# Graph layer on one core: edge sums with destinations as rows, half of each batch in two fp32r parts, mix by token

## The reference

```python
xn = layernorm(x)                                   # (6250, 256)
# graph part: one message per edge, summed at its destination
all_msg = einsum('nf,rfo->rno', xn, weight)         # 16 relations
gate = sigmoid(einsum('nf,rf->rn', xn, gate_weight))
msg = all_msg[rel, src] * norm * gate[rel, src]     # norm: one number per edge
agg = relu(segment_sum(msg, dst))
# mix: linear attention; it folds into one 256 x 256 matrix M
k, v = inst_norm(xn @ w_k), inst_norm(xn @ w_v)     # 8 heads of 64
dots = k.T @ v                                      # per head, over all nodes
mix = (xn @ w_q) @ dots / n @ w_out + b_out         # = xn @ M + b_out
x = x + agg + mix
# ffn: 8 experts, top 2 by a softmax router
y = layernorm(x)
x = x + y + sum_e combine[:, e] * (gelu(y @ w1[e] + b1[e]) @ w2[e] + b2[e])
```

## Time and profile before

| | |
|---|---|
| median of three runs | 1878.89 us |
| profiled execution | 1881.19 us, span 1878.9 us |
| TensorE matmul busy | 1792.0 us, 95% |
| VectorE busy | 1174.8 us, 63% |
| ScalarE busy | 772.5 us, 41% |
| GpSimd busy | 774.0 us, 41%, all of it from 617 us on but a few us |
| granted TensorE clock, mean | 0.984 |

### The profile page before, as it was taken

One profiled execution on the slowest core, in us unless ns is written; L12 is line 12 of the kernel. 1 busy time (PEld: TensorE's weight loads), 2 busy tenths in 40 slices (PEclk: granted clock), 3 DMA queues, 4 the chain that ended last, 5 costly groups with the idle time before them and its releaser, 6 DMA issues.

```text
span 1878.9 us, 30569 instructions
## 1 busy us (share of the span) xinstructions
PE 1792.0 (95%) x11137; PEld 1604.8 (85%) x11137; DVE 1174.8 (63%) x3496; ACT 772.5 (41%) x1428; POOL 774.0 (41%) x812
## 2 busy tenths in 40 slices
PE   5999999999999799999699999999999999999988
PEld 4887888888888699998689998999899989999988
DVE  6555555444443677676657677676686776767764
ACT  4545556555554433332033333333343342432443
POOL 2000000000000466767776666666566666566600
PEclk8999999999999999999899999999999999999999
DMA  7655777655555764443443333433334333333400
GB/s 221 228 222 216 278 291 283 243 213 219 218 219 209 257 244 142 144 146 113 147 123 113 109 121 89 131 112 110 115 94 135 110 108 109 93 118 114 113 16 17
DMA packets 113913, 296.04 MB, mean 158 GB/s; under 512 B 18120, under 2 KB 73792, under 8 KB 104420
## 3 DMA queue, kind: packets, MB, share of 16 engines
q1 hardware_dynamic: 75236, 189.63, 27.4%
q0 software_dynamic: 38528, 104.46, 19.2%
HBM read 162.70 MB, written 131.32 MB: 156 GB/s over the span
## 4 chain that ended last, share of the span: by engine, by line
PE 87%; DVE 6%; POOL 2%; issue 2%; DMA 1%; SPq 1%; ACT 1%; DVEq 0%; ACTq 0%
PE bank L51 22%; PE bank L53 21%; PE bank L52 21%; PE bank L1337 16%; POOL plain L585 2%; PE bank L1326 2%; PE bank L1402 1%; PE bank L1230 1%; DVE plain L951 1%; SPq L479 1%; PE bank L1442 1%; PE bank L1205 1%; DVE plain L984 1%; PE bank L1383 1%; PE bank L1392 0%
## 5 line engine op out<-in xcount | busy, mean ns | idle before, releaser
L585 POOL DMA_INDIRECT plain<-messages,idxT x784 | 763.2, 973 | 1005.5 <-issue 843.2
L51 PE MATMUL bank<-parts 128*128 128x512 f32 (+2 forms) x2232 | 813.3, 364 | 29.5 <-DVE plain L984 21.3
L53 PE MATMUL bank<-parts 128*128 128x512 f32 (+2 forms) x2232 | 786.3, 352 | 0.0
L52 PE MATMUL bank<-parts 128*128 128x512 f32 (+2 forms) x2232 | 785.6, 352 | 0.0
L51 PEld LDWEIGHTS bank<-parts 128*128 128x128 f32 x2232 | 426.6, 191 | 81.9 <-issue 33.7
L53 PEld LDWEIGHTS bank<-parts 128*128 128x128 f32 x2232 | 425.1, 190 | 55.0
L52 PEld LDWEIGHTS bank<-parts 128*128 128x128 f32 x2232 | 426.6, 191 | 46.3
L1337 PE MATMUL bank<-plain 128*128 128x128 f32 x3136 | 392.7, 280 | 22.1 <-DMA plain<-messages,idxT 18.4
L1337 PEld LDWEIGHTS bank<-plain 128*128 128x128 f32 x3136 | 378.1, 196 | 28.6 <-DMA plain<-messages,idxT 20.7
L1156 ACT ACTIVATE plain<-bank,small 128x512 f32<-128x512 f32 (+1 forms) x208 | 135.1, 662 | 376.8 <-PE bank L53 373.4
L658 DVE TENSOR_SCALAR plain<-bank,plain 128x256 f32<-128x256 f32 x392 | 171.0, 478 | 163.0 <-PE bank L53 109.4
(11 more groups left out here) (150 smaller groups left out, 985.3 us busy)
## 6 DMA issues: line engine op xcount, KB each, us to landing
messages<-plain SPq DMA_DIRECT2D x49, 2048.0 KB, 7.0
parts<-xnT_scratch SPq DMA_DIRECT2D x20, 1024.0 KB, 5.1
xnT_scratch<-parts SPq DMA_DIRECT2D x98, 128.0 KB, 3.2
plain<-messages,idxT POOLq DMA_INDIRECT x784, 2.8
w_parts<-parts SPq DMA_DIRECT2D x32, 256.0 KB, 2.4
parts<-w_parts SPq DMA_DIRECT2D x4, 2048.0 KB, 20.4
plain<-in_x SPq DMA_DIRECT2D x48, 128.0 KB, 7.1
plain<-in_x SPq DMA_DIRECT2D x10, 512.0 KB, 4.4
```

The lines of the kernel that those rows point to most:

```text
L51: e.matmul(out, left(0), right(0), start=start, stop=False)
L52: e.matmul(out, left(0), right(1), start=False, stop=False)
L53: return e.matmul(out, left(1), right(0), start=False, stop=stop)
L585: e.indirect_dma_start(msg[:, b % SLOTS, j, :], None, table_rows, bass.IndirectOffsetOnAxis(idxT[:, j, b:b + 1], 0)).then_inc(s_gather[b % ...
```

## The change

1. **Rows for columns.** The one-hot is now the stationary operand and the message chunk (256 features) the moving one. The sum has destinations as partitions, like every other tile of tokens. `agg` becomes [128 partitions, 49 tiles, 256].
2. **Two batches share a sum.** Batches 2i-1 and 2i add into the same PSUM bank and are added to `agg` once, at a row that is a constant of the program (`ROW0`, steps of 64 rows); where the row is 64 the add is in two halves of 64 partitions, into two tiles. The column offset read from memory is gone.
3. **Half of a batch in two parts.** For chunks 0 and 1 the one-hot holds plain ones and zeros (one `tensor_tensor` for both) as fp32r; ScalarE writes the message times norm, rounded to fp32r, in `msg_high` (`high_messages`), VectorE writes what is left in `msg_low` (`low_messages`), and TensorE does one fp32r matmul with each. Chunks 2 and 3 stay f32, with the norm in the one-hot.
4. **Mix by token.** `mix` makes xn x M directly with tokens as partitions, two tiles at a time, with the bias as a matmul with one row (`one_p`, `bout_p`) ahead of it. VectorE adds relu(agg) and x in `agg` itself (`add_mix`). `mix_back`, its transposes, ScalarE's copy, `acc` and `xT` are gone; `xnT` and x are loaded for two tiles at a time.
5. **Norm on ScalarE.** `norm_tile` moves from VectorE to ScalarE (scale and bias form), with one more small VectorE instruction for the bias.
6. `enough` asks for two batches fewer; `w_out` is loaded at `fold` 0 and no longer ahead of the second half; arrays are placed otherwise.

```diff
@@ order
     def enough(g):
-        return BATCHES if START[g + 1] == TILES else -(-START[g + 1] * P * E // N // BATCH) + LAG
+        return min([b for b in range(BATCHES) if ROW0[PAIR_OF[b]] >= START[g + 1] * P] + [BATCHES])
@@ VectorE
             def one_hot(b):
                 if b >= HOTS:
                     e.wait_ge(s_sum_batch, b - HOTS + 1)
-                for j in range(CHUNKS):
-                    m = e.tensor_scalar(onehot[:, b % HOTS, j, :], iota[:, :], offT[:, j, b:b + 1], nrmT[:, j, b:b + 1],
-                                        ALU.is_equal, ALU.mult)
+                e.tensor_tensor(onehot[:, b % HOTS, :, :], iota[:, :].unsqueeze(1).to_broadcast([P, SPLIT, P]),
+                                offT[:, 0:SPLIT, b:b + 1].to_broadcast([P, SPLIT, P]), ALU.is_equal)
+                for j in range(SPLIT, CHUNKS):
+                    m = e.tensor_scalar(onehot_norm[:, b % HOTS, j - SPLIT, :], iota[:, :], offT[:, j, b:b + 1],
+                                        nrmT[:, j, b:b + 1], ALU.is_equal, ALU.mult)
                 m.then_inc(s_onehot, 1)
+            def low_messages(b):
+                e.wait_ge(s_msg_high, b + 1)
+                for j in range(SPLIT):
+                    m = e.scalar_tensor_tensor(msg_low[:, b % SLOTS, j, :], msg[:, b % SLOTS, j, :], nrmT[:, j, b:b + 1],
+                                               raw(msg_high[:, b % HIGHS, j, :]), ALU.mult, ALU.subtract)
+                m.then_inc(s_msg_low, 1)
+            def add_pair(i):
+                e.wait_ge(s_sum_batch, min(2 * i + 1, BATCHES))
...
+                t, row = divmod(ROW0[i], P)
+                spans = [(0, P, t)] if row == 0 else [(row, P, t), (0, row, t + 1)]
+                for r0, r1, t_ in spans:
+                    if t_ < TILES:
+                        m = e.tensor_tensor(agg[r0:r1, t_, :], agg[r0:r1, t_, :], bank[i % 2][r0:r1, 0:D], ALU.add)
@@ VectorE, step "batch"
-                    if b + HOTS - 1 < BATCHES:
-                        one_hot(b + HOTS - 1)
-                    add_batch(b)
+                    if b + LOOK < BATCHES:
+                        one_hot(b + LOOK)
+                        low_messages(b + LOOK)
+                    if b % 2 == 0 or b == BATCHES - 1:
+                        add_pair(PAIR_OF[b])
@@ ScalarE
+            def high_messages(b):
+                e.wait_ge(s_gather[b % SLOTS], 16 * CHUNKS * (b // SLOTS + 1))
+                if b >= HIGHS:
+                    e.wait_ge(s_sum_batch, b - HIGHS + 1)
+                for j in range(SPLIT):
+                    m = e.activation(msg_high[:, b % HIGHS, j, :], msg[:, b % SLOTS, j, :], ACT.Copy, scale=nrmT[:, j, b:b + 1])
+                m.then_inc(s_msg_high, 1)
@@ TensorE
             def sum_batch(b):
-                e.wait_ge(s_gather[b % SLOTS], 16 * CHUNKS * (b // SLOTS + 1))
+                e.wait_ge(s_msg_low, b + 1)
                 e.wait_ge(s_onehot, b + 1)
-                for h in range(KH):
-                    for j in range(CHUNKS):
-                        m = e.matmul(bank[b % 2][:, h * P:(h + 1) * P], msg[:, b % SLOTS, j, h * P:(h + 1) * P],
-                                     onehot[:, b % HOTS, j, :], start=j == 0, stop=j == CHUNKS - 1)
+                for j in range(SPLIT):
+                    e.matmul(bank[i % 2][:, 0:D], onehot[:, b % HOTS, j, :], msg_high[:, b % HIGHS, j, :],
+                             start=first and j == 0, stop=False)
+                    e.matmul(bank[i % 2][:, 0:D], onehot[:, b % HOTS, j, :], msg_low[:, b % SLOTS, j, :], start=False, stop=False)
+                for j in range(SPLIT, CHUNKS):
+                    m = e.matmul(bank[i % 2][:, 0:D], onehot_norm[:, b % HOTS, j - SPLIT, :], msg[:, b % SLOTS, j, :],
+                                 start=False, stop=last and j == CHUNKS - 1)
@@ TensorE, mix of tiles 2p and 2p+1 of a group
+                for k in range(2 * p, min(2 * p + 2, SIZE[g])):
+                    o = bank[3][:, (k % 2) * D:(k % 2 + 1) * D]
+                    for i in range(2):
+                        e.matmul(o, one_p[0:1, :], bout_p[0:1, i, :], start=i == 0, stop=False)
+                    for q in range(KH):
+                        m = three(e, o, lambda i: xnT_g[:, i, q, (k % 2) * P:(k % 2 + 1) * P], lambda i: mix_p[:, i, q, :],
+                                  False, q == KH - 1)
```

More of the change, by code:

```diff
@@ L18 @@
 BATCH = CHUNKS * P
-WINDOW = P
 GROUP = 4
@@ L100, in group_count, with mix_rows, mix_count @@
     def group_count(g):
-        return 16 * sum(parts_of(i) for i in range(g % 2, g + 1, 2))
-    order, closed, opened_to = [], [], 0
+        return 16 * sum(parts_of(i) for i in range(g + 1))
+    MIXES = [(g, p) for g in range(GROUPS) for p in range(-(-SIZE[g] // 2))]
+    def mix_rows(g, p):
+        first, last = START[g] + 2 * p, START[g] + min(2 * p + 2, SIZE[g])
+        whole = min(last, N // P)
+        return [(first, whole)] * (whole > first) + [(whole, last)] * (whole < last)
+    def mix_count(m):
+        return 16 * sum(len(mix_rows(*i)) for i in MIXES[:m + 1])
+    order, placed = [], 0
     def batches_to(n):
-        for b in range(len(closed), min(n, BATCHES)):
-            closed.append(START[opened_to] * P)
+        nonlocal placed
+        for b in range(placed, min(n, BATCHES)):
             order.append(("batch", b))
+        placed = max(placed, min(n, BATCHES))
     def more(n=1):
-        batches_to(len(closed) + n)
+        batches_to(placed + n)
     def enough(g):
-        return BATCHES if START[g + 1] == TILES else -(-START[g + 1] * P * E // N // BATCH) + LAG
+        return min([b for b in range(BATCHES) if ROW0[PAIR_OF[b]] >= START[g + 1] * P] + [BATCHES])
     def ready(g, i):
-        nonlocal opened_to
         if i == 0:
             batches_to(enough(g))
-            opened_to = g + 1
             order.append(("mix", g, 0))
-        elif i == 1:
-            order.append(("mix_back", g, 0))
-        elif i == 2:
+        elif i == 3 and SIZE[g] > 2:
             order.append(("mix", g, 1))
-        elif i == 3:
-            order.append(("mix_back", g, 1))
         elif i == 4:
@@ L278, in gps_layer @@
         route_p = parts.carve(KH, 2, X)
-        parts.at = piece_at
-        piece_p = parts.carve(2, 2, BANK)
+        bout_p = parts.carve(2, D)
+        one_p = parts.carve(P)
+        with nc.sbuf_tensor("piece_parts", [P, 2, 2, BANK], F32R) as piece_p:
+            pass
+        with nc.sbuf_tensor("squares", [P, VK], F32) as sq_t:
+            pass
+        sq = sq_t[:, :]
+        mixes = Arena(sb("mix_parts", [P, 2048], F32R), 2048)
+        mix_p = mixes.carve(2, KH, D)
+        xnT_g = mixes.carve(2, KH, 2 * P)
         parts.at = 0
@@ L285, in gps_layer @@
         h_p = parts.carve(2, 2, KH, GROUP * P)
-        plain = Arena(sb("plain", [P, 23000], F32), 23000)
+        PLAIN = 23424
+        AGG = TILES * D
+        MSG = SLOTS * CHUNKS * D
+        HOT = HIGHS * SPLIT * D + HOTS * CHUNKS * P
+        REST = PLAIN - AGG - MSG - HOT
+        with nc.sbuf_tensor("plain", [P, PLAIN], F32) as held:
+            plain = Arena(held, PLAIN)
+        agg = sb("agg", [P, TILES, D])
+        with nc.sbuf_tensor("msg", [P, SLOTS, CHUNKS, D], F32) as msg:
+            pass
+        msg_low = sb("msg_low", [P, SLOTS, CHUNKS, D], F32R)
+        msg_high = sb("msg_high", [P, HIGHS, SPLIT, D], F32R)
+        onehot = sb("onehot", [P, HOTS, SPLIT, P], F32R)
+        onehot_norm = sb("onehot_norm", [P, HOTS, CHUNKS - SPLIT, P])
+        rest = Arena(sb("rest", [P, REST]), REST)
+        onehot_g = msg[:, 1, :, 0:P]
         stage = plain.carve(2, R, D)
@@ L903, in turn_norm @@
                 for k in ks:
-                    m = e.tensor_tensor(acc[:, s, k, :], acc[:, s, k, :], x3[:, k % 2, :], ALU.add)
+                    m = e.tensor_tensor(agg[:, START[g] + k, :], agg[:, START[g] + k, :], x3[:, k % 2, :], ALU.add)
                 m.then_inc(s_acc, 1)
-                if i == 0:
-                    for k in range(2, SIZE[g]):
-                        norm_tile(g, k)
             def route(g):
@@ L1176, in scalar_program @@
                     e.copy(mix_p[:, 0, :, :], bank[2][:, :].rearrange("p (h o) -> p h o", h=KH)).then_inc(s_mix_high, 1)
-                elif step == "mix":
-                    mix_copy(*a)
+                elif step == "batch":
+                    if a[0] == 0:
+                        for i in range(LOOK):
+                            high_messages(i)
+                    if a[0] + LOOK < BATCHES:
+                        high_messages(a[0] + LOOK)
                 elif step == "norm":
```

364 lines of the change are left out of this document (166 added, 198 removed).

## The result

The changed kernel took 1874.97 us (median of 8, 1872.95 to 1876.67) against 1879.62 of the kernel before (8 runs): ratio 0.9971, 95% interval 0.9961 to 0.9981. Forecast were 1837 us and a range from 1811 to 1866. So there is a gain that can be told from none, 4.7 us, but it is a ninth of the one predicted, and the time lies outside the range.

A forecast was written before the change was run, and what follows sets the result against it. TensorE was taken as the bound, except GpSimd's gathers from 876 to 946 us. From the profiled 1881.2 us, -57 - 9 + 12 + 8 + 4 = -42 gave 1839, as a median 1837 us; range for 8 in 10: 1811 to 1866.

The forecast's parts named there:

- batches: Third stretch, 946 to 1792 us: edge sums on TensorE shorter in 138 batches, 57 us less in all.
- mix, 45 tiles: Mix on TensorE: a group of four tiles takes 4.0 us instead of 3.6, +4 us over the groups.
- matmuls at the low clock: TensorE behind route waits: matmuls run at half clock for a while, 3 us added for longer waits.
- TensorE's waits: Third stretch: 9 us more waiting at 11 routes and 8 us from late gathers, copies and VectorE work.
- The batch's price: One batch's sum on TensorE: 1.38 us instead of 1.79, 0.41 less, or 0.31 less at the other price.
- The wait behind each route: TensorE at 11 routes: two batches shorten by 0.82 us, VectorE's chain doesn't, so waits grow by that, 9 us.
- Queueing: Third stretch: uneven batches queue, late gathers now meet ScalarE and VectorE in order; +8 us, bounds 0 and 30.
- The first two stretches: Before 946 us, 58 batches: GpSimd's gathers set the floor, so only 9 us less, bounds 0 and 18.
- Rival 2: Third stretch: queueing gives half back through VectorE's strict order and ScalarE's copies; 1855 to 1871 us, chance 22%.
- its mark of over 60 us of waits: Sign for the queueing rival: TensorE's waits from the first `up` on exceed 60 us.
- Rival 3: Gathers stopped by VectorE's two-input instructions make GpSimd's pace the bound; about 1950 us, slower, chance 5%.
- the forecast's own marks: Signs expected: TensorE waits 35 to 45 us instead of 18, first `up` about 936 us, mean clock above 0.98.

The follow-up runs named there:

- m1: Changed kernel without the two one-row bias matmuls of a mixed tile (result lacks b_out): 1853.98 us, against 1875.42 for the changed kernel beside it.
- m2: Changed kernel with a mixed tile's two bias matmuls over 128 rows, all but one zero, instead of one row: 1864.76 us, against 1875.42 for the changed kernel.
- s3: Changed kernel with three chunks of a batch split in two parts instead of two: 1907.02 us, against 1874.34 for the changed kernel beside it.
- s1: Changed kernel with one chunk of a batch split in two parts instead of two: 1871.92 us, against 1874.34 for the changed kernel beside it.
- b1: Kernel before with an expert's y_add ahead of the preparation step instead of behind it: 1853.40 us, 0.9847 of the kernel before.
- m3: Changed kernel with y_add ahead of the preparation step, one chunk split and bias matmuls over 128 rows: 1830.56 us, 0.9739 of the kernel before.
- c3: Changed kernel without VectorE's low parts, TensorE multiplying the high part twice (sums lack low parts): 0.9894 of the kernel before.
- c1: Changed kernel with an expert's y_add ahead of the preparation step instead of behind it: 0.9825 of the kernel before.

## Why the prediction was wrong, step by step

From first to last route the forecast's terms, for its 141 batches, against what the starts in TensorE's timeline show, changed less before:

| term | forecast | measured | how read |
|---|---|---|---|
| batches | -58 | -61 | 195.0 - 255.9, the delay of the matmul behind a batch included |
| mix, 45 tiles | +4 | +21 | 60.2 - 39.5, or 45 x (1.34 - 0.88) |
| matmuls at the low clock | +3 | +11 | time above that of the same matmul at the full clock: 5.9 before, 17.2 now |
| TensorE's waits | +17 | +28 | 25.3 before, 52.9 now |
| sum | -34 | -1 | measured -0.4 |

*The batch's price* was right, if anything a little too high (the measured saving is 0.43 us a batch, 0.41 were forecast). *The mix* is the single term that failed most, by 17 us: I took the matmul of a 16-row operand (0.14) as the nearest row for one of one row and left out that those of the earlier trace rows had followed their like. m1 and m2 show that it is on the path and that the one row is the cause.

*TensorE's waits* for VectorE, with the low clock behind them, failed by 19 us together: +20 were forecast (9 behind the routes, 8 of queueing, 3 of clock), +39 measured. The wait behind each route was right in sort and too small. The step that failed is "Those two batches get 0.82 us shorter and the chain doesn't, so the wait grows by this much": at 1164 the wait grew by 1.94 us, not by 0.82. The chain itself is as long as it was (5.9 us from its copy to y_add), but VectorE came to it late: its 1.66 us of slack were used up by what it has more to do for the batches, 0.47 us each by the forecast's own prices. So the wait ends when it did, at 1164.2, though TensorE had come 1.9 us earlier. The waits also came where none were forecast. Of those above 1 us for y_add, eleven now stand behind the routes, 26 us together (four and 8.5 us before), and eight at other experts, 15 us (two and 2.2 us before).

*The clock*: seven waits of 2.5 us or more inside this stretch were each overlapped or soon followed by a stretch at the lower level (granted clock 0.5); of the fourteen shorter ones above 1 us one was. In the kernel before it was so with four of its five waits of 2.2 us and more. s3 shows both together: 83 us of waits, clock 0.95.

*Queueing* (+8): GpSimd did slow down as expected in kind (983 to 1051 ns a gather), but TensorE does not wait for low parts here (1.0 us). The queueing shows as y_add's wait instead, as I read it. What of VectorE's lateness is its amount of work and what is order can't be parted wholly: both levers work, s1 and s3 for the amount, b1 for the order in the kernel before, m3 for the order in the changed kernel together with two edits. By these sums only the amount is new: the bad place of y_add cost the kernel before 26 us already and costs the changed one 26 to 32. VectorE is 78% busy and still late, since it is late at given places.

*The first two stretches* (-9; 3.6 measured, the first `up` at 941.90 instead of 945.54): the 216 gathers from the first that waits end in 277.2 instead of 288.5 us, but they begin 3.7 us later (655.21 against the earlier trace rows's 651.54), and from the last of them to the `up` 9.5 us pass instead of 5.6: here ScalarE's copy, the route's chain on VectorE and the low part stand one behind another. I had 1.6 us for this way. In this stretch the waits for low parts appear, 19.4 us in seven.

*The rivals.* Rival 2 gave the mechanism (queueing gives it back; its mark of over 60 us of waits was nearly met, 53), and its time, up to 1871, was too low with the mix. Its sum doesn't follow from its conditions either: two more microseconds at 11 routes and gathers at 30 us instead of 8 make -42 + 22 + 22, so about 1881, and the text gives no reason for its -4. Rival 3 needed gathers over 1.2 us; they are at 1.05. Of the forecast's own marks the waits (35 to 45), the first `up` (936) and the clock (above 0.98, now 0.975) told of the miss.

## What to carry to other kernels

Work taken from a full TensorE is worth only what the engines that feed it can follow at each place, not on average: look which instruction ends TensorE's longest waits and what stands ahead of it on its own engine; moving that one (here y_add by one step) gave 26 us in the kernel before, more than the whole change. An engine that waits for the full one has slack there; work added to it is free only up to that slack (here 1.66 us at a route). Price a new operation by a row of the same shape and in the same company: a one-row matmul between full ones took 0.31 us with what it delays, not 0.14. And charge the longer waits of TensorE (here those of 2.5 us or more) with the matmuls at the low clock behind them.

## What the runs showed of the hardware

- Two matmuls whose stationary operand has one row cost 0.62 us amid full ones (1.34 - 0.72 a tile); with 128 rows, 127 of them zero, 0.24. Their weight load started 0.31 us behind the preceding matmul's start instead of with it.
- f32 matmuls of 256 columns, four records a pair of chunks, take 0.167 us from start to start in a row, less than twice the 0.112 of 128 columns; but the fp32r matmul behind them is 0.19 us late, which was 0.09 behind those of 128 columns.
- Mean issue time of a gather grew with the low parts, VectorE instructions that read two operands in SBUF: 982 (kernel before), 1025, 1051, 1113 ns with none, one, two and three a batch, and over the whole span it was 984 ns without them, with ScalarE's copies kept (c3), against 1029 beside it in the same set (c1). Why they slow it, no run shows.
